# The second attention's exponentials turned by VectorE's 32x32 squares and a trip through HBM, in place of TensorE's transposes

## The chip, the core and the metric

The kernel runs on one core of a Trainium2 chip. The metric is the device time of one execution in microseconds, as a median over runs. A core has five engines that work side by side, each through its own instructions in program order: TensorE (PE, matrix products), VectorE (DVE), ScalarE (ACT), GpSimd (POOL) and SyncE (SP), which here only issues DMAs. They wait for one another through semaphores.

## What is computed

Sixteen images x of 256 channels by 1024 positions. A convolutional attention block, then on the 1024 tokens t of 256 channels:

```python
xn      = group_norm(x, 8 groups) * w + b
q, k, v = split(qkv_w @ xn + qkv_b)
x       = x + proj_w @ (softmax(q^T k / 16) v) + proj_b      # first attention, 1024 x 1024
t       = tokens(x)
u       = layer_norm(t)
c       = u / |u|
t       = t + softmax((c c^T) ** 2) u                        # second attention, 1024 x 1024
t       = t + round(clip(layer_norm(t) @ sign(W) * g + bias, -1, 1) * 7) / 7
```

The scores c c^T of the second attention are symmetric, and so are their squares' exponentials, E. Only their lower triangle is computed; the upper one is its transpose.

## The kernel before

A loop runs over the 16 images, called batches (b). 1024 tokens are 8 tiles (NT) of 128 (P). Every float32 product is made of three fp32r matmuls: a "hi" part rounded to fp32r and a "lo" part, what the rounding left out; hi x hi, hi x lo and lo x hi are added. So each operand costs a copy (hi) and a subtraction (lo).

`front(b, f)` does the group norm products, the first attention, the layer norm and the second attention's scores of batch b, with the last steps of batch f = b - 1 between them; `back(b)` does the second attention's eight products. Each engine has its own `front` and `back`, which are the order of its queue, written out by hand.

First attention: eight rows of exponentials in `expo` (four slots, DEEP). For rows 0 to 6 VectorE's `e1_turn` (line 1032) transposes within squares of 32x32 into `e_turned`, which is the memory of `x_norm`; SP's `send` and `fetch` (lines 351, 361) write that to HBM and read it back into `e_back` so that the squares stand in their transposed places; ScalarE's `e1T_hi` (766) and VectorE's `e1T_lo` (1037) split it.

Second attention: row J of E has the columns 0 to (J+1)*128. TensorE's `scores2(b, u)` makes it (row 7 as two halves, u = 7 and 8), ScalarE's `exp2` squares and exponentiates it into `expo` (822, 824), VectorE's `e2_hi` (1072) casts it into `prob[:, 0]`, and GpSimd's `e2_lo` (1333, rows 0 to 6) or VectorE's `e2_last_lo` (1077, row 7) subtracts into `prob[:, 1]`. For its blocks i < J, TensorE's `turn_e2(b, J)` (565) transposes J blocks of 128x128 into the PSUM tensor `turn`; VectorE's `e2T_parts` (1083, 1085) copies and subtracts them from there into column tile J of rows 0 to J-1 of `prob`. `product2(b, n)` then sums over j the block (j, n) of `prob` with `val`: 8 j's of three matmuls of 256 or 258 columns, into one of four PSUM places. product2(0) waits for each row's low part as it comes (`p_made`, `p_last_made`), product2(n) for `pT_made` of row n. `turn_cos` (535) and `cosT_lo` (1066) make the operands of the scores. VectorE's `residual2(n)` adds product2(n) to the tokens and takes statistics; GpSimd's and ScalarE's `layer_norm2` follow.

In `back`, the next batch is begun: ScalarE's `normalise` and `norm_hi` write `x_norm` and its hi part, GpSimd's `norm_lo` (1289) the lo part, and `bias_quads` (1338) adds a bias in `e_back`. `x_tok` holds x by tokens: written early in `front` (1009), read by `residual1` (1055) for the last time before the second attention's transposes.

Of the kernel before, what the change touches and what calls it, by code (L numbers as in the profile page):

```python
# [34 lines left out]
P = 128  # L35
# [10 lines left out]
def build(nc, x, norm_w, norm_b, qkv_w, qkv_b, proj_w, proj_b, ffn_w, ffn_b, out):  # L46
# [17 lines left out]
    GROUP_OF = [g for g, (n0, n1) in enumerate(GROUPS1) for _ in range(n0, n1)]  # L64
    assert KC == 2 and N == 2 * BANK and C // GROUPS == 32
# [6 lines left out]
    with ExitStack() as ctx:  # L72
# [62 lines left out]
        e_scratch = nc.dram_tensor("e_scratch", (NT, P, N), F32).ap()  # L135
        e_in = e_scratch.rearrange("n (i j) (q f) -> n q j i f", i=SQ, q=SQ)
# [118 lines left out]
        pT_up = sem("pT_up")  # L255
        pT_hi_made = sem("pT_hi_made")
        pT_made = sem("pT_made")
# [47 lines left out]
        def turned(J):  # L305

            first = J % 2 * BANK if J <= HT else 0
            return turn[:, first:first + J * P]


        @block.sync
        def _(sp):
# [49 lines left out]

            def front(b, f):
# [20 lines left out]
            reload_quads(1)  # L384
            with sp.Fori(1, B - 1) as b:
                reload(b + 1)
                front(b, b - 1)
                reload_quads(b + 1)
            front(B - 1, B - 2)
            store(B - 1, 0)  # L390
# [6 lines left out]
        def _(pe):  # L397
# [160 lines left out]
            def turn_e2(b, J):  # L558
                if J < 3:
                    pe.wait_ge(eT_last_made, b + 1)  # L560
                else:
                    pe.wait_ge(pT_made, (NT - 1) * b + (J - 2 if J <= HT else J - 1))
                pe.wait_ge(e2_made, NP * b + (J + 1 if J < NT - 1 else NP))
                for i in range(J):
                    mm = pe.transpose(turned(J)[:, tile(i)], expo[:, J % DEEP, tile(i)], ident[:, :])
                mm.then_inc(pT_up, 1)

            def product2(b, n):
# [7 lines left out]
                if n:  # L576
                    pe.wait_ge(pT_made, (NT - 1) * b + n)
                else:
                    pe.wait_ge(val_made, N1 * b + N1)
                def block_parts(j):  # L580
                    if n == 0 and j < NT - 1:
                        pe.wait_ge(p_made, (NT - 1) * b + j + 1)
                    elif n in (0, HT) and j == NT - 1:
                        pe.wait_ge(p_last_made, 2 * b + 1 + n // HT)
                    return prob[:, 0, j, tile(n)], prob[:, 1, j, tile(n)]

                mm = product(out2[n % 4], block_parts,
                             lambda j: val[:, j, 0:C + 2], lambda j: val[:, j, C + 2:2 * C + 2])
# [27 lines left out]
            def front(b, f, more):  # L616
# [96 lines left out]
            for n in range(NT - 2):  # L713
                product2(f, n)
                if n == 2:
                    turn_e2(f, NT - 1)
            pe.wait_ge(pT_made, (NT - 1) * B)
# [12 lines left out]
        def _(act):  # L730
            def normalise(b, k, again):
                act.wait_ge(gn_scale, b + 1)
                if again:
                    act.wait_ge(e1_written[k], 16 * SENT_OF[k] * b)
# [75 lines left out]
            def exp2(b, u):  # L810
# [8 lines left out]
                if J > DEEP:  # L819
                    act.wait_ge(pT_up, (NT - 1) * b + J - DEEP)  # L820
# [3 lines left out]
                act.activation(e, e, ACT.Exp).then_inc(e2_made, 1)  # L824

# [14 lines left out]
            def front(b, f, more, reuse=True):  # L840
# [81 lines left out]
            f = B - 1  # L922
            for n in range(NT - 3):
# [507 lines left out]
```

## Time and profile before

| | us |
|---|---|
| median of 3 runs (1765.05 to 1765.96) | 1765.87 |
| the profiled execution, its own time | 1766.2 |
| span of its core, first to last instruction | 1764.5 |
| TensorE busy | 1727.6 |
| VectorE busy | 1385.3 |
| ScalarE busy | 935.3 |
| GpSimd busy | 769.2 |

Times of single instructions come from this one profiled execution. Busy times of pipelined matmuls overlap each other, so the time that a run of them takes is read start to start from the timeline. An engine's idle time is listed with what ended it. The timeline rows used are of the batch that runs from 881.0 to 988.9 us; the batches between the first and the last look alike.

### The profile page before, as it was taken

The page shows a single profiled execution, that of the slowest core. Times are in us where ns is not written, and L with a number is a line of the kernel's source. Part 1 is how long each engine was busy: PE and PEld are TensorE (multiplying, and loading weights), DVE is VectorE, ACT ScalarE, POOL GpSimd, SP SyncE. Part 2 cuts the span into 40 slices and gives each one's busy share as a digit, 9 for nine tenths or more (in the row PEclk, how much of TensorE's full clock was granted, in tenths as well). Part 3 has the DMA queues.
Part 4 walks back from the last instruction along what each step waited for, and adds up shares of the span by engine and source line. Part 5 has one row for each costly group of instructions (what it writes and reads, how often), then busy time and mean ns, then how long its engine had stood idle before and what let it go on. Part 6 is the DMA issues. An engine that isn't in the chain of part 4 may idle for free.

```text
span 1764.5 us, 34002 instructions
## 1 busy us (share of the span) xinstructions
PE 1727.6 (98%) x11682; PEld 1578.8 (89%) x11682; DVE 1385.3 (79%) x2597; ACT 935.3 (53%) x1444; POOL 769.2 (44%) x1206
## 2 busy tenths in 40 slices
PE   7999999999999999999999999999999999999997
PEld 5898989989899998999989999898998989999896
DVE  7778877788777887778788787887778877788775
ACT  3555646455464554735547365564645546455472
POOL 1362615427154372634626246271552715437161
PEclk9999999999999999999999999999999999999998
DMA  4604315042250613406133160431504325061320
GB/s 129 167 25 137 103 51 163 24 157 81 75 139 24 186 52 100 114 36 195 31 121 95 58 178 24 135 103 50 164 24 155 83 74 140 24 187 28 103 90 25
DMA packets 139551, 169.67 MB, mean 96 GB/s; under 512 B 13184, under 2 KB 121088, under 8 KB 139520
## 3 DMA queue, kind: packets, MB, share of 16 engines
q1 hardware_dynamic: 139520, 169.27, 32.6%
q8 instruction: 18, 0.29, 0.1%
q14 instruction: 13, 0.11, 0.0%
HBM read 93.72 MB, written 75.50 MB: 96 GB/s over the span
## 4 chain that ended last, share of the span: by engine, by line
issue 27%; POOL 26%; PE 25%; DVE 7%; ACT 7%; DMA 6%; SPq 1%; POOLq 1%; DVEq 0%; ACTq 0%
PE wide L402 12%; POOL xn_lo L1289 4%; POOL ln_r L1299 4%; POOL prob L1333 4%; POOL e_back L1338 3%; PE turn L604 3%; DMA e_scratch<-x_norm 3%; DMA e_back<-e_scratch 3%; PE narrow L402 2%; POOL val L1325 2%; ACT expo L759 2%; PE turn L595 2%; POOL sq_root L1313 1%; DVE x_norm L1032 1%; DVE prob L1015 1%
## 5 line engine op out<-in xcount | busy, mean ns | idle before, releaser
L402 PE MATMUL wide<-xn_hi,prob 128*128 128x512 f32 x1024 | 305.5, 400 | 3.1 <-DVE prob L1015 3.1
L800 ACT ACTIVATE ln<-tok,ln_shift,ln_r 128x256 f32<-128x256 f32 x128 | 68.4, 592 | 303.8 <-POOL ln_shift L1301 303.8
L402 PEld LDWEIGHTS wide<-xn_hi,prob 128*128 128x128 f32 x1024 | 185.5, 188 | 44.7 <-DVE prob L1015 6.4
L1296 POOL TENSOR_TENSOR ln_v<-ln_mv,ln_eps 128x2 f32<-128x2 f32 (+1 forms) x112 | 22.1, 198 | 417.4 <-DVE ln_mv L1060 234.7
L1349 POOL TENSOR_TENSOR carrier_p<-ones 128x1 f32<-128x1 f32 x60 | 11.7, 195 | 417.2 <-DVE y_sb L1108 414.7
L766 ACT ACTIVATE prob<-e_back 128x1024 fp32r<-128x1024 f32 x112 | 118.3, 1056 | 139.6 <-DMA e_back<-e_scratch 139.6
L759 ACT ACTIVATE expo<-wide,neg_max 128x1024 f32<-128x1024 f32 x128 | 142.5, 1113 | 73.9 <-DVE neg_max L1025 73.3
L1032 DVE STREAM_TRANSPOSE x_norm<-expo 128x1024 f32<-128x1024 f32 x112 | 139.2, 1243 | 41.1 <-ACT expo L759 40.6
L1333 POOL TENSOR_TENSOR prob<-expo,prob 128x128 fp32r<-128x128 f32 (+6 forms) x112 | 148.6, 1339 | 45.8 <-DVE prob L1072 45.8
L1025 DVE TENSOR_REDUCE neg_max<-wide 128x1 f32<-128x1024 f32 x128 | 155.3, 1214 | 13.5 <-PE wide L402 11.7
L1037 DVE TENSOR_TENSOR prob<-e_back,prob 128x1024 fp32r<-128x1024 f32 x112 | 136.1, 1215 | 33.5 <-ACT prob L766 33.5
L402 PE MATMUL wide<-xn_lo,prob 128*128 128x512 f32 x512 | 160.7, 394 | 0.0
L495 PE MATMUL narrow<-val,prob 128*128 128x258 f32 x512 | 150.1, 293 | 0.0
L495 PE MATMUL narrow<-prob 128*128 128x256 f32 x512 | 147.7, 289 | 1.7 <-DVE prob L1037 1.7
L495 PE MATMUL wide<-prob 128*128 128x256 f32 x512 | 148.7, 290 | 0.0
L495 PE MATMUL wide<-val,prob 128*128 128x258 f32 x512 | 147.0, 287 | 0.0
L497 PE MATMUL narrow<-prob 128*128 128x256 f32 x512 | 145.4, 284 | 0.0
L496 PE MATMUL narrow<-prob 128*128 128x256 f32 x512 | 145.3, 284 | 0.0
L497 PE MATMUL wide<-val,prob 128*128 128x258 f32 x512 | 145.0, 283 | 0.0
L497 PE MATMUL narrow<-val,prob 128*128 128x258 f32 x512 | 144.9, 283 | 0.0
L497 PE MATMUL wide<-prob 128*128 128x256 f32 x512 | 144.8, 283 | 0.0
L496 PE MATMUL wide<-prob 128*128 128x256 f32 x512 | 144.7, 283 | 0.0
(179 smaller groups left out, 5488.9 us busy)
## 6 DMA issues: line engine op xcount, KB each, us to landing
e_scratch<-x_norm SPq DMA_DIRECT2D x112, 512.0 KB, 3.0
e_back<-e_scratch SPq DMA_DIRECT2D x448, 128.0 KB, 3.2
x_raw<-in_x SPq DMA_DIRECT2D x32, 512.0 KB, 3.7
e_back<-in_x SPq DMA_DIRECT2D x64, 256.0 KB, 5.0
out<-y_sb SPq DMA_DIRECT2D x64, 256.0 KB, 3.0
tok<-in_L_conv_qkv_w SPq DMA_DIRECT2D x1, 768.0 KB, 6.4
ln<-in_L_conv_proj_w SPq DMA_DIRECT2D x1, 256.0 KB, 6.4
ln<-in_L_ffn_weight SPq DMA_DIRECT2D x1, 256.0 KB, 3.7
```

Of the source, the lines that this page charges most:

```text
L402: mm = pe.matmul(o, lhsT, r, start=first and i == 0, stop=last and i == len(parts) - 1)
L495: pe.matmul(o[:, 0:w], hi, value_hi(j), start=j == 0, stop=False)
L496: pe.matmul(o[:, 0:C], hi, value_lo(j), start=False, stop=False, skip_group_check=True)
L497: mm = pe.matmul(o[:, 0:w], lo, value_hi(j), start=False, stop=j == NT - 1)
L759: act.activation(expo[:, n % DEEP], wide[n % 2][:, :], ACT.Exp, bias=neg_max[:, n:n + 1], accum_out=row_sum1[:, n:n + 1]).then_inc(e1_made, 1)
L766: act.activation(eT_hi[n].rearrange("p (n i t) -> p n i t", n=NT, i=SQ), e_back[:, n % 2].rearrange("p i (n t) -> p n i t", n=NT), ACT.Cop ...
L1025: dve.tensor_reduce(neg_max[:, n:n + 1], wide[n % 2][:, :], AX.X, ALU.max, negate=True).then_inc(max_made, 1)
L1032: dve.transpose(e_turned[:, n % 2].rearrange("p (q n t) -> p n q t", q=SQ, n=NT), expo[:, n % DEEP].rearrange("p (n q t) -> p n q t", q=SQ ...
L1037: dve.tensor_sub(eT_lo[n].rearrange("p (n i t) -> p n i t", n=NT, i=SQ), e_back[:, n % 2].rearrange("p i (n t) -> p n i t", n=NT), eT_hi[n ...
L1289: pool.tensor_sub(xn_lo[:, k], x_norm[:, k], xn_hi[:, k].bitcast(F32)).then_inc(xn_lo_made, 1)
L1299: pool.tensor_tensor(inv[:, cols], v[:, cols], minus_half[:, one], ALU.pow).then_inc(steps, 1)
L1333: pool.tensor_sub(prob[:, 1, J, row], expo[:, J % DEEP, row], prob[:, 0, J, row].bitcast(F32)).then_inc(p_made, 1)
```

## The change

TensorE's `turn_e2`, the PSUM reads of `e2T_parts` and their semaphores go. In their place, for rows J = 1 to 7 in five groups (1, 2), (3, 4), (5), (6), (7): VectorE's `e2_turn(b, J)` transposes the J blocks of `expo` within squares of 32x32 into a slot of `e_turned`; SP's `send2` writes a group to HBM and `fetch2` reads it back in four pieces of 32 partitions into `e2_back`, a slot in the memory of `x_tok`; ScalarE's `e2T_hi` and VectorE's `e2T_lo` split it into `prob`. Groups use two slots in turn; a fetch from the third group on waits until the slot's last group is split. `product2` waits, for j < n, for the group of row n. Its matmuls are otherwise the same, with j in the order 0 to 7 for every n. `normalise` of the next batch waits until the last group of its slot is written, as it overwrites `e_turned`, and stands among the `e2T_hi` in ScalarE's order. Left out below are declarations of semaphores and the first and last batch's copies of the same orders.

```diff
     GROUP_OF = [g for g, (n0, n1) in enumerate(GROUPS1) for _ in range(n0, n1)]
+    E2G = [(1, 2), (3, 4), (5,), (6,), (7,)]
+    E2_OF = [len(E2G) // 2, (len(E2G) + 1) // 2]
...
         e_scratch = nc.dram_tensor("e_scratch", (NT, P, N), F32).ap()
+        e2_scratch = nc.dram_tensor("e2_scratch", (len(E2G), P, (NT - 1) * P), F32).ap()
+        e2_flat = x_tok[:, :, :].rearrange("p n c -> p (n c)")
...
-        def turned(J):
-
-            first = J % 2 * BANK if J <= HT else 0
-            return turn[:, first:first + J * P]
...
+        def e2_count(b, g):
+
+            return E2_OF[e2_slot(g)] * b + g // 2 + 1
...
+        def e2_sent(g):
+
+            return e_turned[:, e2_slot(g), 0:e2_width(g) * P]
+
+        def e2_back(g):
+
+            first = e2_slot(g) * N
+            return e2_flat[:, first:first + e2_width(g) * P]
...
+            def send2(b, g):
+                sp.wait_ge(e2_turned, (NT - 1) * b + E2G[g][-1])
+                sp.dma_start(e2_scratch[g, :, 0:e2_width(g) * P], e2_sent(g)).then_inc(e2_written[e2_slot(g)], 16)
+
+            def fetch2(b, g):
+                due = 16 * e2_count(b, g)
+                sp.wait_ge(e2_written[e2_slot(g)], due)
+                if g >= 2:
+                    sp.wait_ge(e2T_made[e2_slot(g)], due)
+                source = e2_scratch[g, :, 0:e2_width(g) * P].rearrange("(i t) (q f) -> q t i f", t=Q, q=SQ)
+                back = e2_back(g).rearrange("p (i f) -> p i f", i=SQ)
+                for q in range(SQ):
+                    sp.dma_start(back[q * Q:(q + 1) * Q], source[q]).then_inc(e2_landed[e2_slot(g)], 16)
+
+            def second(b):
+                send2(b, 0)
+                fetch2(b, 0)
+                send2(b, 1)
+                send2(b, 2)
+                fetch2(b, 1)
+                send2(b, 3)
+                fetch2(b, 2)
+                send2(b, 4)
+                fetch2(b, 3)
+                fetch2(b, 4)
...
-            def turn_e2(b, J):
-                if J < 3:
-                    pe.wait_ge(eT_last_made, b + 1)
-                else:
-                    pe.wait_ge(pT_made, (NT - 1) * b + (J - 2 if J <= HT else J - 1))
-                pe.wait_ge(e2_made, NP * b + (J + 1 if J < NT - 1 else NP))
-                for i in range(J):
-                    mm = pe.transpose(turned(J)[:, tile(i)], expo[:, J % DEEP, tile(i)], ident[:, :])
-                mm.then_inc(pT_up, 1)
+            def product2_parts(b, n, j, order):
+                if j < n:
+                    g = E2G_OF[n]
+                    pe.wait_ge(e2T_made[e2_slot(g)], 16 * (e2_count(b, g) + 1))
+                hi, lo = prob[:, 0, j, tile(n)], prob[:, 1, j, tile(n)]
+                w = C + 2
+                o = out2[n % 4]
+                pe.matmul(o[:, 0:w], hi, val[:, j, 0:w], start=j == order[0], stop=False)
+                pe.matmul(o[:, 0:C], hi, val[:, j, w:w + C], start=False, stop=False, skip_group_check=True)
+                return pe.matmul(o[:, 0:w], lo, val[:, j, 0:w], start=False, stop=j == order[-1])
...
-                if n:
-                    pe.wait_ge(pT_made, (NT - 1) * b + n)
-                else:
                     pe.wait_ge(val_made, N1 * b + N1)
-                def block_parts(j):
+                if n == HT:
+                    pe.wait_ge(p_last_made, 2 * b + 2)
+                for j in range(NT):
                     if n == 0 and j < NT - 1:
                         pe.wait_ge(p_made, (NT - 1) * b + j + 1)
-                    elif n in (0, HT) and j == NT - 1:
-                        pe.wait_ge(p_last_made, 2 * b + 1 + n // HT)
-                    return prob[:, 0, j, tile(n)], prob[:, 1, j, tile(n)]
-
-                mm = product(out2[n % 4], block_parts,
-                             lambda j: val[:, j, 0:C + 2], lambda j: val[:, j, C + 2:2 * C + 2])
+                    elif n == 0:
+                        pe.wait_ge(p_last_made, 2 * b + 1)
+                    mm = product2_parts(b, n, j, range(NT))
...
                 scores2(b, 3)
-                turn_e2(b, 1)
-                turn_e2(b, 2)
                 scores2(b, 4)
-                turn_e2(b, 3)
                 turn_cos(b, 3)
                 scores2(b, 5)
-                turn_e2(b, 4)
                 scores2(b, 6)
-                turn_e2(b, 5)
                 scores2(b, 7)
                 scores2(b, 8)
-                turn_e2(b, 6)
...
                 for n in range(NT):
                     product2(b, n)
-                    if n == 2:
-                        turn_e2(b, NT - 1)
...
             def normalise(b, k, again):
                 act.wait_ge(gn_scale, b + 1)
                 if again:
-                    act.wait_ge(e1_written[k], 16 * SENT_OF[k] * b)
+                    act.wait_ge(e2_written[k], 16 * E2_OF[k] * b)
                 act.activation(by_tile(x_norm[:, k]), by_quad(x_raw[:, k]), ACT.Identity, bias=gn_b[:, k:k + 1],
                                scale=gn_a[:, k:k + 1]).then_inc(xn_made, 1)
...
                 if J > DEEP:
-                    act.wait_ge(pT_up, (NT - 1) * b + J - DEEP)
+                    act.wait_ge(e2_turned, (NT - 1) * b + J - DEEP)
...
+            def e2T_hi(b, J):
+                g, m = E2G_OF[J], e2_first(J)
+                act.wait_ge(e2_landed[e2_slot(g)], 16 * SQ * e2_count(b, g))
+                back = e2_back(g).rearrange("p (i n t) -> p n i t", i=SQ, t=Q)[:, m:m + J]
+                act.activation(prob[:, 0, 0:J, tile(J)].rearrange("p n (i t) -> p n i t", i=SQ), back, ACT.Copy
+                               ).then_inc(e2T_hi_made, 1)
...
                 exp2(b, 6)
                 exp2(b, 7)
                 exp2(b, 8)
+                e2T_hi(b, 1)
+                e2T_hi(b, 2)
 
             def back(b, more):
-                if more:
-                    for k in range(KC):
-                        normalise(b + 1, k, again=True)
-                        norm_hi(b + 1, k, again=True)
+                e2T_hi(b, 3)
+                e2T_hi(b, 4)
+                normalise(b + 1, 0, again=True)
+                norm_hi(b + 1, 0, again=True)
+                e2T_hi(b, 5)
+                normalise(b + 1, 1, again=True)
+                norm_hi(b + 1, 1, again=True)
+                e2T_hi(b, 6)
+                e2T_hi(b, 7)
...
+            for J in range(3, NT):
+                e2T_hi(f, J)
...
-            def e2T_parts(b, J):
-                up = turned(J).rearrange("p (i t) -> p i t", i=J)
-                dve.wait_ge(pT_up, (NT - 1) * b + J)
-                dve.tensor_copy(prob[:, 0, 0:J, tile(J)], up).then_inc(pT_hi_made, 1)
-                dve.wait_ge(pT_hi_made, (NT - 1) * b + J)
-                dve.tensor_sub(prob[:, 1, 0:J, tile(J)], up, prob[:, 0, 0:J, tile(J)].bitcast(F32)
-                               ).then_inc(pT_made, 1)
+            def e2_turn(b, J):
+                g, m = E2G_OF[J], e2_first(J)
+                dve.wait_ge(e2_made, NP * b + (J + 1 if J < NT - 1 else NP))
+                if g < 2:
+                    dve.wait_ge(e1_written[e2_slot(g)], 16 * SENT_OF[e2_slot(g)] * (b + 1))
+                else:
+                    dve.wait_ge(e2_written[e2_slot(g)], 16 * (e2_count(b, g) - 1))
+                dve.transpose(e2_sent(g).rearrange("p (q n t) -> p n q t", q=SQ, t=Q)[:, m:m + J],
+                              expo[:, J % DEEP, 0:J * P].rearrange("p (n q t) -> p n q t", q=SQ, t=Q)
+                              ).then_inc(e2_turned, 1)
+
+            def e2T_lo(b, J):
+                g, m = E2G_OF[J], e2_first(J)
+                dve.wait_ge(e2T_hi_made, (NT - 1) * b + J)
+                back = e2_back(g).rearrange("p (i n t) -> p n i t", i=SQ, t=Q)[:, m:m + J]
+                low = dve.tensor_sub(prob[:, 1, 0:J, tile(J)].rearrange("p n (i t) -> p n i t", i=SQ), back,
+                                     prob[:, 0, 0:J, tile(J)].rearrange("p n (i t) -> p n i t", i=SQ).bitcast(F32))
+                if J == E2G[g][-1]:
+                    low.then_inc(e2T_made[e2_slot(g)], 16)
...
                 cosT_lo(b, 2)
+                e2_turn(b, 1)
                 e2_hi(b, 2)
-                e2T_parts(b, 1)
-                e2T_parts(b, 2)
+                e2_turn(b, 2)
                 e2_hi(b, 3)
+                e2_turn(b, 3)
                 cosT_lo(b, 3)
-                e2T_parts(b, 3)
                 e2_hi(b, 4)
-                e2T_parts(b, 4)
+                e2_turn(b, 4)
                 e2_hi(b, 5)
-                e2T_parts(b, 5)
+                e2_turn(b, 5)
                 e2_hi(b, 6)
+                e2_turn(b, 6)
                 e2_hi(b, 7)
                 e2_last_lo(b, 7)
-                e2T_parts(b, 6)
                 e2_hi(b, 8)
+                e2_turn(b, 7)
+                e2T_lo(b, 1)
+                e2T_lo(b, 2)
                 e2_last_lo(b, 8)
 
             def back(b):
-                for n in range(NT):
-                    if n == 2:
-                        e2T_parts(b, NT - 1)
+                e2T_lo(b, 3)
+                e2T_lo(b, 4)
+                residual2(b, 0)
+                residual2(b, 1)
+                e2T_lo(b, 5)
+                residual2(b, 2)
```

## Rows read from the trace of the kernel before

**Rows 1.** The page, part 1 (busy us, share, instructions) and clock by slices.

```profile
PE 1727.6 (98%) x11682; PEld 1578.8 (89%) x11682; DVE 1385.3 (79%) x2597; ACT 935.3 (53%) x1444; POOL 769.2 (44%) x1206
...
PEclk9999999999999999999999999999999999999998
```

**Rows 2.** Groups of instructions by shape: busy us, mean ns, idle before.

```profile
L565 PE MATMUL turn<-ident,expo 128*128 128x128 f32 x448 | 64.5, 272 | 0.0
```

**Rows 3.** Timeline, TensorE, one batch: start us, length us, engine, line, op, out<-in.

```profile
881.00 0.62 PE L402 MATMUL wide<-xn_hi,qk_lo 128*128 128x512 f32 x2
...
954.40 0.49 PE L565 MATMUL turn<-ident,expo 128*128 128x128 f32 x3
...
955.18 0.63 PE L535 MATMUL narrow<-ident,cos_x 128*128 128x128 f32 x4 [0.30 <-ACT cos_x L795]
...
963.95 0.82 PE L565 MATMUL turn<-ident,expo 128*128 128x128 f32 x6
964.52 0.37 PE L495 MATMUL narrow<-val,prob 128*128 128x258 f32 x1
...
967.42 0.39 PE L495 MATMUL narrow<-val,prob 128*128 128x258 f32 x1
...
967.88 0.28 PE L495 MATMUL narrow<-val,prob 128*128 128x258 f32 x1
...
973.66 0.93 PE L565 MATMUL turn<-ident,expo 128*128 128x128 f32 x7
...
988.87 0.62 PE L402 MATMUL wide<-xn_hi,qk_lo 128*128 128x512 f32 x2
```

**Rows 4.** Timeline, VectorE, same batch.

```profile
958.59 0.48 DVE L1072 CAST prob<-expo 128x640 fp32r<-128x640 f32 x1
...
960.31 0.82 DVE L1072 CAST prob<-expo 128x768 fp32r<-128x768 f32 x1
...
962.99 1.83 DVE L1072 CAST prob<-expo 128x896 fp32r<-128x896 f32 x2
964.86 2.51 DVE L1077 TENSOR_TENSOR prob<-expo,prob 128x512 fp32r<-128x512 f32 x1
```

**Rows 5.** Timeline, VectorE, last batch.

```profile
1724.00 0.69 DVE L1077 TENSOR_TENSOR prob<-expo,prob 128x512 fp32r<-128x512 f32 x1
```

**Rows 6.** Timeline, GpSimd, same batch.

```profile
955.22 2.46 POOL L1333 TENSOR_TENSOR prob<-expo,prob 128x384 fp32r<-128x384 f32 x2
959.15 1.57 POOL L1333 TENSOR_TENSOR prob<-expo,prob 128x640 fp32r<-128x640 f32 x1 [1.47 <-DVE prob L1072]
960.68 1.51 POOL L1325 TENSOR_TENSOR val<-ln_x,val 128x512 fp32r<-128x512 f32 x1
962.15 1.85 POOL L1333 TENSOR_TENSOR prob<-expo,prob 128x768 fp32r<-128x768 f32 x1
964.57 2.24 POOL L1333 TENSOR_TENSOR prob<-expo,prob 128x896 fp32r<-128x896 f32 x1 [0.56 <-DVE prob L1072]
```

**Rows 7.** Timeline, ScalarE, same batch as rows 3.

```profile
960.85 0.92 ACT L822 ACTIVATE expo<-wide 128x896 f32<-128x896 f32 x1 [1.22 <-PE wide L402]
```

**Rows 8.** Groups by shape: square transposes, xn_lo, bias.

```profile
L1032 DVE STREAM_TRANSPOSE x_norm<-expo 128x1024 f32<-128x1024 f32 x112 | 139.2, 1243 | 41.1 <-ACT expo L759 40.6
...
L1289 POOL TENSOR_TENSOR xn_lo<-x_norm,xn_hi 128x1024 fp32r<-128x1024 f32 x30 | 74.2, 2495 | 14.6 <-ACT xn_hi L742 14.6
...
L1338 POOL TENSOR_TENSOR e_back<-e_back,quad_bias 128x1024 f32<-128x1024 f32 x32 | 67.2, 2120 | 8.4 <-DVE quad_bias L1130 8.4
```

**Rows 9.** The page, part 6: DMA issues, KB each, us from issue to landing.

```profile
e_scratch<-x_norm SPq DMA_DIRECT2D x112, 512.0 KB, 3.0
e_back<-e_scratch SPq DMA_DIRECT2D x448, 128.0 KB, 3.2
```

**Rows 10.** Stretches of prologue and tail: us, busy PE, PEld, DVE, ACT, POOL (instructions), clock, DMA.

```profile
25.00:26.00 1.00, 0.00 (x0) 0.00 (x0) 0.96 (x3) 1.00 (x1) 0.07 (x1) 1.00 0.00 0
1747.00:1751.00 4.00, 1.35 (x11) 0.87 (x9) 1.00 (x2) 3.33 (x5) 0.22 (x2) 1.00 0.00 0
1751.50:1754.50 3.00, 2.53 (x6) 2.04 (x7) 2.86 (x5) 0.00 (x0) 0.00 (x0) 0.50 0.00 0
```

More of the change, by code:

```diff
@@ L64, in build @@
     GROUP_OF = [g for g, (n0, n1) in enumerate(GROUPS1) for _ in range(n0, n1)]
+    E2G = [(1, 2), (3, 4), (5,), (6,), (7,)]
+    E2_OF = [len(E2G) // 2, (len(E2G) + 1) // 2]
+    E2G_OF = {J: g for g, rows in enumerate(E2G) for J in rows}
     assert KC == 2 and N == 2 * BANK and C // GROUPS == 32
@@ L254, in build @@
         p_last_made = sem("p_last_made")
-        pT_up = sem("pT_up")
-        pT_hi_made = sem("pT_hi_made")
-        pT_made = sem("pT_made")
+        e2_turned = sem("e2_turned")
+        e2_written = [sem("e2_written0"), sem("e2_written1")]
+        e2_landed = [sem("e2_landed0"), sem("e2_landed1")]
+        e2T_hi_made = sem("e2T_hi_made")
+        e2T_made = [sem("e2T_made0"), sem("e2T_made1")]
         pv2_up = sem("pv2_up")
@@ L303, in offset, with e2_slot, e2_width, e2_first @@
             return P if (J + 1) * P == BANK + P else 0
-        def turned(J):
-            first = J % 2 * BANK if J <= HT else 0
-            return turn[:, first:first + J * P]
+        def e2_slot(g):
+            return (g + 1) % 2
+        def e2_count(b, g):
+            return E2_OF[e2_slot(g)] * b + g // 2 + 1
+        def e2_width(g):
+            return sum(E2G[g])
+        def e2_first(J):
+            return sum(i for i in E2G[E2G_OF[J]] if i < J)
+        def e2_sent(g):
[3 more added lines that the diff above has]
+            return e2_flat[:, first:first + e2_width(g) * P]
         @block.sync
@@ L384, in _ @@
             reload_quads(1)
+            second(0)
             with sp.Fori(1, B - 1) as b:
@@ L388, in _ @@
                 reload_quads(b + 1)
+                second(b)
             front(B - 1, B - 2)
+            second(B - 1)
             store(B - 1, 0)
@@ L714, in _ @@
                 product2(f, n)
-                if n == 2:
-                    turn_e2(f, NT - 1)
-            pe.wait_ge(pT_made, (NT - 1) * B)
             turn_ln2(f, 0, LAST)
@@ L1198, in front @@
                 cosT_lo(b, 2)
+                e2_turn(b, 1)
                 e2_hi(b, 2)
-                e2T_parts(b, 1)
-                e2T_parts(b, 2)
+                e2_turn(b, 2)
                 e2_hi(b, 3)
+                e2_turn(b, 3)
                 cosT_lo(b, 3)
-                e2T_parts(b, 3)
                 e2_hi(b, 4)
-                e2T_parts(b, 4)
+                e2_turn(b, 4)
                 e2_hi(b, 5)
-                e2T_parts(b, 5)
+                e2_turn(b, 5)
                 e2_hi(b, 6)
+                e2_turn(b, 6)
                 e2_hi(b, 7)
                 e2_last_lo(b, 7)
-                e2T_parts(b, 6)
                 e2_hi(b, 8)
+                e2_turn(b, 7)
+                e2T_lo(b, 1)
+                e2T_lo(b, 2)
                 e2_last_lo(b, 8)
             def back(b):
-                for n in range(NT):
-                    if n == 2:
-                        e2T_parts(b, NT - 1)
+                e2T_lo(b, 3)
[4 more added lines that the diff above has]
+                residual2(b, 2)
+                e2T_lo(b, 6)
+                residual2(b, 3)
+                e2T_lo(b, 7)
+                for n in range(HT, NT):
                     residual2(b, n)
@@ L1233, in _ @@
             f = B - 1
-            for n in range(NT - 2):
-                if n == 2:
-                    e2T_parts(f, NT - 1)
-                residual2(f, n)
+            e2T_lo(f, 3)
+            e2T_lo(f, 4)
+            residual2(f, 0)
+            residual2(f, 1)
+            e2T_lo(f, 5)
+            residual2(f, 2)
+            e2T_lo(f, 6)
+            residual2(f, 3)
+            e2T_lo(f, 7)
+            residual2(f, 4)
+            residual2(f, 5)
             ln2T_lo(f, 0, LAST)
@@ L1255, in prepare @@
                 pool.memset(half[:, :], 0.5).then_inc(eT_made[1], 16)
-                pool.memset(minus_one[:, :], -1.0)
-                pool.memset(ln_eps[:, :], LN_EPS)
+                pool.memset(minus_one[:, :], -1.0).then_inc(e2T_made[0], 16)
+                pool.memset(ln_eps[:, :], LN_EPS).then_inc(e2T_made[1], 16)
                 pool.memset(norm_eps[:, :], NORM_EPS)
```

## The prediction

> **What bounds the kernel now.** Busy time first: TensorE is busy 98% of the span, VectorE 79% [rows 1]. The granted clock is 9 tenths or more except in the last slice [rows 1]. So TensorE's own work is the span, as long as it stays fed. Then the group that the change deletes: 448 transposes, 64.5 us of busy time [rows 2]. They are pipelined, so busy time overstates them; the timeline of one batch gives their true price. Its queries start at 881.00, those of the next at 988.87: a period of 107.9 us [rows 3]. Last I read who is late around those transposes, on each engine, because an instruction taken out of TensorE's queue gives time back only where the next one is ready.
>
> **What the deleted transposes really cost TensorE.** Start to start, six take 964.52 - 963.95 = 0.57 us, 0.095 each [rows 3]. 28 per batch are 2.7 us, with some 0.08 for the restart of the matmul behind each of six blocks 3.2 us. Over 16 batches 51 us: the number that a reader of the busy table would expect.
>
> **Where it is not given back.** (a) Blocks J=1 and 2 stand before score row 4, and block J=3 (954.40) before turn_cos(3), which still idled 0.30 us for ScalarE's cos_x and started at 955.18 [rows 3]. ScalarE's order up to there isn't touched, so turn_cos(3) stays where it is and the first three blocks give nothing. (b) Blocks 4, 5 and 6, 15 transposes, give 15 x 0.095 and restarts, about 1.55 us: product2(0) starts at about 962.95 in place of 964.52 [rows 3]. But product2(0) needs in its last steps e2_lo(6) (GpSimd) and e2_last_lo(7) (VectorE); at present its eighth step starts at 967.42, right behind the VectorE op that ends at 964.86 + 2.51 = 967.37 [rows 3, 4]. (c) Only the block of seven, from 973.66, lies in a stretch where TensorE is the only limit. From product2(1)'s start to the next queries is 988.87 - 967.88 = 20.99 us; seven products of 24 matmuls at 0.12 are 20.2. So 0.79 us returns there.
>
> **The chain that decides: the lows of rows 4 to 7.** VectorE and GpSimd hold each other up where VectorE casts from SBUF or subtracts with both operands in SBUF. e2_last_lo of 512 columns takes 0.69 us with GpSimd idle [rows 5] and 2.51 us beside e2_lo(6), ending 0.56 us after GpSimd does at 964.57 + 2.24 = 966.81 [rows 4, 6]. The cast of row 6 started at 962.99, waited until e2_lo(5) ended at 964.00, and e2_lo(6) followed at 964.57.
>
> Now the new order. e2_hi(4) stands directly behind cosT_lo(3); it is held only by e2_lo(2) and (3), which end at 955.22 + 2.46 = 957.68, and ends at 958.1, where at present it begins at 958.59 [rows 4, 6]. So e2_lo(4) starts at 958.2, not 959.15: ends 959.75. e2_hi(5), ready at 959.65, goes first then: 960.2. value_lo(3): 961.25 (1.06 after the cast, as before). e2_lo(5), 1.85 us: 963.05 [rows 6]. e2_hi(6): its exponential is done at about 962.3 (ScalarE starts it at 960.85, right behind score row 6 [rows 7]; now 0.44 earlier, 1.9 long), so e2_lo(5) decides: 963.55. e2_lo(6), 2.24: 965.85. Here the change puts e2_turn(6) between e2_hi(6) and e2_hi(7). A square transpose of 1024 columns takes 1.243 us [rows 8]; with 0.07 fixed and 0.135 per 128 columns, as issued back to back (an estimate; no shorter one is in the trace), row 6 costs 0.88 and row 7 1.02. So e2_hi(7) arrives at 964.4, when GpSimd is in e2_lo(6), and waits until 965.85. At present it slips in ahead of e2_lo(6). Then e2_hi(7), e2_last_lo(7): 966.8. product2(0) ends at 967.3, against 967.88: 0.6 us earlier.
>
> **What product2(1) now waits for.** It needs the group of rows 1 and 2 back and split. The data are there: e2_turn(2), early in VectorE's order, is done by about 953.3, a write takes 3.0 us and a read 3.2 [rows 9], with four issues about 8.5 us, landed by 962. But e2T_lo(1) and (2) stand in VectorE's order behind e2_hi(8) and e2_turn(7): 966.7 + 0.34 + 1.02 + 0.21 + 0.42 gives 968.7. So product2(1) starts at 968.75, 0.87 us later than before. With the 0.79 of (c), the batch is longer by about 0.1 us. Of the 3.2 us nothing is left; TensorE is idle instead: 0.8 before the seventh step of product2(0), 0.55 before the eighth, 1.45 before product2(1), 2.8 us of 3.65 from 965.1 to 968.75.
>
> **What else moves, and its cover.** The seven copies of the squares' upper parts go from VectorE to ScalarE; VectorE gets seven transposes of nearly the same length for them: load about level. The low parts now read SBUF, so they can be held by GpSimd's xn_lo (2.5 us) and bias (2.1 us) [rows 8]. Worked through with trip times as above: rows 3, 4 done at 970.4 (needed 974.5); row 5's fetch waits for the slot that e2T_lo(2) frees at 968.7, lands 973.2, done 974.7 (needed 980.3); row 6 done 979.5 (needed 983.2); row 7, whose fetch waits for row 5's slot, lands at 979.1, ScalarE 980.1, VectorE held by the bias op 982.6 (needed 986.1). Least slack 3.4 us: costed at nothing. normalise of the next batch waits for the last write (about 973.9); xn_lo ends near 978.7 against 989: nothing. On SP the x reload follows the last fetch (976.4), needed 20 us later. ScalarE's and GpSimd's last layer norm rows stay tied to product2(7). The 28 more waits before matmuls of product2 are on passed semaphores; product2(0) has eight such waits now at a pitch of 0.12 us: nothing.
>
> The Trainium skill (VectorE: DVE Perf Modes, "Rules for kernel authors") speaks against this edit: it sends a 128x128 transpose to TensorE where PSUM will do, and leaves VectorE its 32x32 squares. TensorE's 0.095 us [rows 3] stand against 0.15 of VectorE per block of 128 columns [rows 8]; by the rule the change loses, by TensorE's busy row it gains 51 us, and the sum above lies near zero.
>
> **The clock.** A gap of this form has a price that the middle of this trace doesn't show. In the tail TensorE was busy 1.35 us of the 4 us from 1747, and then ran at half the clock (1.2 GHz) in the whole stretch 1751.5 to 1754.5 [rows 10]. In the prologue it was idle for the whole microsecond 25 to 26 and kept 2.4 GHz [rows 10]. The new gap (0.85 busy of 3.65) is emptier than the first and lies inside steady work, once per batch. Half clock for some 3.2 us loses about 1.6 us of TensorE's time, in the products, where it is the limit. Whether it falls in a given batch I take as even: the bounds are no batch (nothing) and 16 batches (26 us); half, 8 x 1.6 = 13 us, because the two rows bracket the gap from both sides.
>
> The Trainium skill (TensorE: Matmul & The Clock Gate, "What's actually happening") says that the slow clock is the default and activity releases it; the tail's rows agree.
>
> **Sum.** Profiled execution of before: span 1764.5, 1766.2 with what lies around it, 0.3 above the median 1765.87. + 16 x 0.1 + 13 = 1780.8; less 0.3: 1780 us.
>
> **Rivals.**
> 1. Same chain, clock stays up: 1764 to 1770, so 1767. For it: gaps of 1 us didn't lower it; against it: 1747 to 1754.5.
> 2. The gap is shorter: if VectorE's chain ends up to 1 us earlier (e2_hi(7) let in before e2_lo(6), or faster transposes), product2(1) starts with product2(0)'s end. 16 x 1 less: 1750. Against it: GpSimd is released by e2_hi(6) itself, 0.9 us before e2_hi(7) can arrive.
> 3. All of it comes back: 1766 - 51 = 1715. It needs VectorE and GpSimd to be off the path, which [rows 3, 4] refute.
> 4. Slower by the trip: the four-piece reads have runs of 384 to 896 bytes, and two trips stand in a row behind e2T_lo(2) (rows 5, then 7). From 1.7 us extra on each trip on, product2(7) waits; at 3 us each it waits 2.6 us, + 42: some 1810 without a clock fall. For it: no row shows so short a run; against it: e_back's 3.2.
>
> **How the numbers follow.** Forecast (gap and clock falls) 0.48, 1772 to 1792; rival 1 0.20; rival 2 0.13; rival 3 0.03; rival 4 0.16. Range 1760 to 1798: the forecast, rival 1, the near part of 2 and of 4, about 0.8. A measurement can tell about 0.2%, 3.5 us, from no change: faster 0.16, same 0.17 (most of rival 1), slower 0.67. Both signs are open only through VectorE's order, so the forecast's own range, 1772 to 1792, is the one to hold it to.
>
> **What would show it.** TensorE's transposes of expo in PSUM fall from 448 to none; product2(0)'s first step at -1.5 us against the scores' start, its last near -0.6; idle before product2(1) near 1.4 us released by VectorE's e2T_lo, in every batch; e2_hi(7) waiting behind e2_lo(6). Clock of some batches at one half for 3 us just behind that gap. No wait of product2(3), (5), (6), (7). It is wrong if product2(1) isn't late, if the clock stays up, or if products 5 to 7 wait for landings.

## The result, and the profile after

The changed kernel takes 1790.53 us (median of four, 1789.10 to 1791.13), the kernel before 1765.46 on the same chip: 1.0141 of it, 95% interval 1.0124 to 1.0159. It is 25 us slower, though TensorE has less to do. The page of the changed kernel, part 1, beside [rows 1]:

```profile
PE 1707.2 (95%) x11234; PEld 1551.0 (87%) x11234; DVE 1347.9 (75%) x2597; ACT 996.2 (56%) x1556; POOL 778.3 (44%) x1206
```

The 448 transposes are gone (11682 to 11234 matmuls), TensorE is busy 20 us less and its share fell from 98 to 95%. In the span of 1788.4 us its waits have new names. From the list of waits of the changed kernel (who waited for whom: total us, times, longest):

```profile
PE narrow L619 <- DVE prob L1151: 20.1, 16, 1.3
...
PE narrow L619 <- POOL prob L1418: 8.6, 16, 0.6
PE wide L456 <- DVE tokT_lo L1122: 8.6, 16, 0.7
...
PE narrow L619 <- DVE prob L1133: 6.2, 16, 0.4
```

Line 1151 is e2T_lo, 1418 e2_lo, 1133 e2_last_lo. Each of these three comes 16 times, once per batch, 34.9 us together. (Line 1122 is cosT_lo; it is taken up under part (a) below.) The timeline of one batch shows where. Its queries start at 892.93, 11.93 us later than those of the batch in [rows 3], so 11.93 is to be taken off to compare. TensorE:

```profile
892.93 0.62 PE L456 MATMUL wide<-xn_hi,qk_lo 128*128 128x512 f32 x2
...
974.92 0.28 PE L619 MATMUL narrow<-val,prob 128*128 128x258 f32 x1
...
976.96 0.28 PE L621 MATMUL narrow<-val,prob 128*128 128x258 f32 x1
977.74 0.39 PE L619 MATMUL narrow<-val,prob 128*128 128x258 f32 x1 [0.51 <-POOL prob L1418]
...
978.09 0.28 PE L621 MATMUL narrow<-val,prob 128*128 128x258 f32 x1
978.75 0.39 PE L619 MATMUL narrow<-val,prob 128*128 128x258 f32 x1 [0.39 <-DVE prob L1133]
...
979.09 0.28 PE L621 MATMUL narrow<-val,prob 128*128 128x258 f32 x1
980.62 0.58 PE L619 MATMUL narrow<-val,prob 128*128 128x258 f32 x1 [1.24 <-DVE prob L1151]
981.00 0.41 PE L620 MATMUL narrow<-val,prob 128*128 128x256 f32 x1
...
1002.21 0.62 PE L456 MATMUL wide<-xn_hi,qk_lo 128*128 128x512 f32 x2
```

product2(0) starts at 974.92, which is 962.99 on the old batch's clock, 1.5 us earlier than in [rows 3]. product2(1) starts at 980.62, which is 968.69 on the old batch's clock, where [rows 3] has 967.88. And its first matmuls take 0.41 us where 0.28 is usual. GpSimd and VectorE in the same stretch, beside [rows 4, 6]:

```profile
969.94 1.56 POOL L1418 TENSOR_TENSOR prob<-expo,prob 128x640 fp32r<-128x640 f32 x1 [0.43 <-DVE prob L1128]
971.47 1.19 POOL L1410 TENSOR_TENSOR val<-ln_x,val 128x512 fp32r<-128x512 f32 x1
973.15 1.85 POOL L1418 TENSOR_TENSOR prob<-expo,prob 128x768 fp32r<-128x768 f32 x1 [0.49 <-DVE prob L1128]
975.57 2.12 POOL L1418 TENSOR_TENSOR prob<-expo,prob 128x896 fp32r<-128x896 f32 x1 [0.56 <-DVE prob L1128]
```

```profile
974.29 1.19 DVE L1128 CAST prob<-expo 128x896 fp32r<-128x896 f32 x1 [0.47 <-ACT expo L864]
975.41 0.96 DVE L1143 STREAM_TRANSPOSE x_norm<-expo 128x768 f32<-128x768 f32 x1
976.30 1.67 DVE L1128 CAST prob<-expo 128x512 fp32r<-128x512 f32 x1
978.00 0.69 DVE L1133 TENSOR_TENSOR prob<-expo,prob 128x512 fp32r<-128x512 f32 x1
978.61 0.42 DVE L1128 CAST prob<-expo 128x512 fp32r<-128x512 f32 x1
978.95 1.10 DVE L1143 STREAM_TRANSPOSE x_norm<-expo 128x896 f32<-128x896 f32 x1
979.98 0.58 DVE L1151 TENSOR_TENSOR prob<-x_tok,prob 128x128 fp32r<-128x128 f32 x2
```

The cast of row 7's first half (976.30) takes 1.67 us, where the same cast takes 0.42 at 978.61: e2_lo(6) on GpSimd runs beside the first until 977.69 and beside the second not at all. Behind it stand the subtraction, a cast, the transpose of row 7, and only then the two lows that product2(1) needs. ScalarE had delivered their hi parts long before:

```profile
976.47 0.60 ACT L870 ACTIVATE prob<-x_tok 128x128 fp32r<-128x128 f32 x2
```

The clock, in stretches of the changed kernel (columns as in rows 10):

```profile
980.00:980.50 0.50, 0.00 (x0) 0.00 (x0) 0.50 (x4) 0.50 (x1) 0.00 (x0) 0.62 0.00 0
980.60:983.20 2.60, 2.58 (x12) 2.59 (x13) 2.53 (x6) 1.14 (x2) 1.27 (x1) 0.50 0.44 96
```

Here it falls in the middle of the idle time before product2(1), at 980.12, and stays at 1.2 GHz for 3.4 us, 2.9 of them in work. Each of the first fifteen batches has a fall close to this place: in the first it begins 1.0 us after product2(1)'s start, then earlier from batch to batch, and from the eighth on about 0.5 us ahead of it. In the fifteenth the clock stays low for 6.8 us. In the sixteenth the three waits are there and the clock doesn't fall. The kernel before has no fall in the second attention; its only ones are at 51.6 us, in the first batch, and in the tail. From one batch's queries to the next's it is 107.8 to 107.9 us before (107.2 the first) and 109.2 to 109.5 after (110.8 the fifteenth).

### The profile page after: what moved, and what is told of

Same layout as the page of the kernel before. It is cut to its first block, busy times and chain, and to the rows that moved or that the text cites. A ratio compares the mean times of both kernels' runs of the same rounds, so it can differ in the third digit from the quotient of the medians.

```text
span 1788.4 us, 33803 instructions
## 1 busy us (share of the span) xinstructions
PE 1707.2 (95%) x11234; PEld 1551.0 (87%) x11234; DVE 1347.9 (75%) x2597; ACT 996.2 (56%) x1556; POOL 778.3 (44%) x1206
## 4 chain that ended last, share of the span: by engine, by line
issue 29%; POOL 25%; PE 22%; DVE 8%; ACT 7%; DMA 6%; SPq 1%; POOLq 1%; DVEq 0%; ACTq 0%
PE wide L456 11%; POOL e_back L1423 4%; POOL ln_r L1384 4%; POOL prob L1418 3%; PE turn L655 3%; DMA e_back<-e_scratch 3%; POOL val L1410 3%; DMA e_scratch<-x_norm 3%; PE narrow L456 2%; ACT expo L799 2%; POOL xn_lo L1374 2%; PE turn L646 2%; DVE x_norm L1088 1%; POOL sq_root L1398 1%; DVE prob L1071 1%
## 5 line engine op out<-in xcount | busy, mean ns | idle before, releaser
L619 PE MATMUL narrow<-val,prob 128*128 128x258 f32 x512 | 161.0, 315 | 34.9 <-DVE prob L1151 20.1
L1081 DVE TENSOR_REDUCE neg_max<-wide 128x1 f32<-128x1024 f32 x128 | 155.2, 1213 | 12.0 <-PE wide L456 10.8
L620 PE MATMUL narrow<-val,prob 128*128 128x256 f32 x512 | 154.2, 301 | 0.0
L621 PE MATMUL narrow<-val,prob 128*128 128x258 f32 x512 | 154.2, 301 | 0.0
L549 PE MATMUL narrow<-prob 128*128 128x256 f32 x512 | 147.3, 288 | 2.5 <-DVE prob L1093 2.5
L549 PE MATMUL wide<-prob 128*128 128x256 f32 x512 | 148.7, 290 | 0.0
L619 PEld LDWEIGHTS narrow<-val,prob 128*128 128x128 f32 x512 | 107.7, 210 | 45.3 <-DVE prob L1151 20.3
L1128 DVE CAST prob<-expo 128x128 fp32r<-128x128 f32 (+2 forms) x144 | 118.3, 831 | 36.5 <-ACT expo L864 36.5
L551 PE MATMUL narrow<-prob 128*128 128x256 f32 x512 | 144.8, 283 | 0.0
```

Source lines behind the costliest of these rows:

```text
L549: pe.matmul(o[:, 0:w], hi, value_hi(j), start=j == 0, stop=False)
L551: mm = pe.matmul(o[:, 0:w], lo, value_hi(j), start=False, stop=j == NT - 1)
L619: pe.matmul(o[:, 0:w], hi, val[:, j, 0:w], start=j == order[0], stop=False)
L620: pe.matmul(o[:, 0:C], hi, val[:, j, w:w + C], start=False, stop=False, skip_group_check=True)
L621: return pe.matmul(o[:, 0:w], lo, val[:, j, 0:w], start=False, stop=j == order[-1])
L1081: dve.tensor_reduce(neg_max[:, n:n + 1], wide[n % 2][:, :], AX.X, ALU.max, negate=True).then_inc(max_made, 1)
```

## Experiments

The theory: TensorE's time that the transposes took was time in which it would have waited for GpSimd and VectorE; what is new is a wait for VectorE's order before product2(1), and the gap costs a clock fall on top. Rivals: the clock is innocent; the trip through HBM comes late; busy time counts after all. The first four ran on one chip beside the kernel before (1764.60 there).

**The gap filled.** In the changed kernel, matmuls that nobody reads, where TensorE idled:

```diff
+                def fill(count):
+                    for _ in range(count):
+                        pe.matmul(turn[:, 0:C], prob[:, 0, 0, tile(0)], val[:, 0, 0:C], start=True, stop=True)
+                if n == 1:
+                    fill(11)
                 for j in range(NT):
+                    if n == 0 and j in (NT - 2, NT - 1):
+                        fill(6 if j == NT - 2 else 4)
```

> The changed kernel, with 21 extra matmuls of 256 columns per batch whose result nobody reads, placed in TensorE's queue where it idled: 6 before the seventh step of product2(0), 4 before the eighth, 11 before product2(1) (each 0.12 us, 2.5 us in all). No wait and no result changes. Theory (the gap lowers TensorE's clock in every batch, 1.4 us each): TensorE stays busy, the clock stays up, the period goes from 109.3 to about 107.9 us and the time to some 1767 us, though TensorE does more work. Rival (the clock is harmless, the 1.4 us per batch are waits or slower steps elsewhere): no shorter than 1790, and up to 40 us longer if the extra matmuls don't fit in the idle time.

Measured: 1769.15 us (1768.52 to 1770.62), 1.0027 of before, interval 1.0017 to 1.0038. With 336 matmuls more it is some 21 us faster than the changed kernel, and the waits for lines 1151, 1418 and 1133 are gone from its list. Period 108.0 us, and the granted clock is 1.00 from the first batch until the tail. From the first queries to the last, fifteen periods, it takes 22.7 us less than the changed kernel: that is what sixteen low stretches of 3.4 us cost, 1.4 each. And it takes 1.9 us more than before, 0.12 per batch: that is what the change costs without the clock. It is a low figure, as before has a fall in its first batch and this kernel has none; from the second batch on the periods are 107.8 and 108.0, a difference of 0.16.

**The two lows ahead.** One move in VectorE's order:

```diff
                 e2_last_lo(b, 7)
+                e2T_lo(b, 1)
+                e2T_lo(b, 2)
                 e2_hi(b, 8)
                 e2_turn(b, 7)
-                e2T_lo(b, 1)
-                e2T_lo(b, 2)
                 e2_last_lo(b, 8)
```

> The changed kernel with e2T_lo(1) and e2T_lo(2) ahead of e2_hi(8) and e2_turn(7) in VectorE's order; nothing else moves. Theory (product2(1) waits for VectorE's order, not for the trip): the wait before product2(1) goes from 1.3 to about 0 us, the gap is then too small for the clock to fall, period about 106.6 us, 1744 us. If the clock still falls in every batch: 108.1 and 1769. Rival (the trip through HBM, or ScalarE's share of it, is what comes late): the wait before product2(1) stays and the time stays near 1790.

Measured: 1748.11 us (1747.23 to 1749.88), 0.9910 of before (0.9893 to 0.9926). Two lines moved make the changed kernel some 41 us faster (0.9910 of before, not 1.0141); the time is 4 us above the 1744 expected. Its list of waits:

```profile
PE narrow L619 <- POOL prob L1418: 8.7, 16, 0.7
...
PE narrow L619 <- DVE prob L1133: 6.2, 16, 0.4
```

The wait for line 1151 is gone, the other two are as they were, and the clock doesn't fall in any batch. Period 106.7 us (107.5 and 107.0 in the second and third). So the data had been there: the wait was for VectorE's order, not for the trip.

**The trip made longer.**

```diff
             def fetch2(b, g):
                 due = 16 * e2_count(b, g)
+                sp.dma_start(pad[g:g + 1, :], x_d[0, 0:1, 0, 0:P]).then_inc(padded, 16)
+                sp.wait_ge(padded, 16 * (len(E2G) * b + g + 1))
```

> The changed kernel with a small HBM to HBM copy of 512 bytes that SP issues and waits for before each of the five fetches: about 2 us more on each trip, in series with what SP does next. Theory (least slack of a landing is 3 us or more and one trip of the two in a row is not enough to use it up): period unchanged within 0.3 us, 1790 to 1795. Rival (the trips are on the path): at least 2 us per batch, 1822 or more.

Measured: 1793.14 us (1791.62 to 1796.79), 1.0170 of before (1.0153 to 1.0187), 2.6 us above the changed kernel's 1790.53. The first two delays of one batch in SP's timeline, each with the write ahead of it, the copy and the fetch:

```profile
1075.78 0.35 SPq L392 DMA_DIRECT2D e_scratch<-x_norm  x1
1076.18 0.58 SPq L396 DMA_DIRECT2D pad<-in_x  x1
1078.14 1.73 SPq L404 DMA_DIRECT2D x_tok<-e_scratch  x4
1081.09 3.68 SPq L392 DMA_DIRECT2D e_scratch<-x_norm  x2
1084.82 0.55 SPq L396 DMA_DIRECT2D pad<-in_x  x1
1086.89 1.75 SPq L404 DMA_DIRECT2D x_tok<-e_scratch  x4
```

From the copy's issue to the fetch's it is 2 us each time, but the first fetch had to wait for its write for most of that anyway. Counted from the batch's queries, the five fetches are issued 0.4, 2.0, 0.6, 3.0 and 2.5 us later than in the changed kernel, and their data land 0.3, 1.7, 0.7, 2.3 and 2.5 us later (medians over the batches). So the experiment delays three of the five trips by about 2 us, the second, fourth and fifth, and hardly the other two. TensorE's waits are those of the changed kernel (20.1, 8.7 and 6.2 us): these three trips are covered with 2 us to spare. It is not much more than that: row 7's low part, whose two trips in a row are both longer, is done 3.2 to 3.7 us before product2(7) in most batches, 2.0 to 2.1 in three of the four without a fall, where TensorE comes sooner, and 0.5 in the fourth. The expected time came true, the unchanged period did not. The periods do something new: 108.0 in four batches, 109.3 to 109.5 in seven, 110.8 in two (and 108.4 and 110.6 in the first two). In the batches of 108.0 the clock doesn't fall; in those of 110.8 it is low for 6.8 us, not 3.4. TensorE's gap is as long as ever, but it no longer lowers the clock each time. The idle time before product2(1) in two batches, and the stretch behind it:

```profile
546.77 0.39 PE L623 MATMUL narrow<-val,prob 128*128 128x258 f32 x1 [1.24 <-DVE prob L1155]
...
1091.19 0.58 PE L623 MATMUL narrow<-val,prob 128*128 128x258 f32 x1 [1.24 <-DVE prob L1155]
```

```profile
546.50:549.50 3.00, 2.73 (x22) 2.73 (x23) 2.89 (x8) 2.89 (x4) 0.00 (x0) 1.00 0.29 66
1091.00:1094.00 3.00, 2.81 (x13) 2.81 (x14) 2.89 (x9) 2.89 (x4) 0.00 (x0) 0.50 0.30 73
```

The two waits ahead of it are 0.52 and 0.38 us in the first batch, 0.51 and 0.39 in the second, so the gap is the same to 0.01 us. Behind the first the clock stays at full speed, behind the second it is at half. So within one kernel and one execution the length of the gap doesn't decide. And these batches without a fall are 1.3 to 1.5 us shorter than those with one, which shows the price of the clock a second time.

**The transposes taken out of the kernel before.** Only the first of each block is done, so upper parts are stale:

```diff
-                for i in range(J):
-                    mm = pe.transpose(turned(J)[:, tile(i)], expo[:, J % DEEP, tile(i)], ident[:, :])
+                mm = pe.transpose(turned(J)[:, tile(0)], expo[:, J % DEEP, tile(0)], ident[:, :])
```

> The kernel before with only one of each block's transposes left: 21 of 28 per batch are not done, so most of the upper parts are stale (part of the computation is left out); all waits, copies and the order stay. Theory (blocks 1 to 6 were done in time in which TensorE would have waited anyway; only the block of seven was on the path, 6 x 0.095): period 107.9 to about 107.3, some 1756 us. Rival (busy time is what counts): 16 x 21 x 0.095 = 32 us less, 1733.

Measured: 1753.80 us (1753.40 to 1755.61), 0.9943 (0.9927 to 0.9960): 10.8 us less, where 21 x 16 x 0.095 = 32 us of transposes were dropped. Period 107.1. In the place of the transposes TensorE waits for GpSimd's e2_lo, 12.4 us in 16 waits, of which the list of before has none. Two thirds of the transposes' time had been cover, as reckoned.

The next four ran on one chip beside before at 1765.11.

**The same gap, elsewhere in time.** To see why the clock fell every time, product2(5) is preceded by 8 matmuls of 256 columns (in the second run by 14), in steady work; the gap isn't touched.

```diff
+                if n == 5:
+                    for _ in range(8):
+                        pe.matmul(turn[:, 0:C], prob[:, 0, 0, tile(0)], val[:, 0, 0:C], start=True, stop=True)
```

> The changed kernel with 8 more matmuls of 256 columns (0.96 us) ahead of product2(5) in every batch, where TensorE is never idle; the gap before product2(1) is as it was. If a gap of this form lowers the clock whenever it comes: one fall in every batch again, periods 110.3, 1806 us. If the fall in every batch was a matter of where the gap lay in time from batch to batch (a period that repeated that): falls in some batches only, periods of 108.9 and 110.3 side by side, 1790 to 1804.

> As e7_add8 with 14 matmuls (1.68 us). Always a fall: periods 111.0, 1817 us. Only where the gap lies right in time: periods of 109.6 and 111.0 side by side, 1800 to 1815.

Measured, one run each: 1810.16 us with 8 and 1805.56 with 14: more work, less time. With 14 that is where the second of the two readings had it. With 8 it is above both (1806, or 1790 to 1804), with the periods side by side that the second reading asked for, but not fewer low stretches. With 8, the periods repeat in threes, 109.0, 111.7, 110.5. Three successive batches, in stretches around and behind the gap (columns as in rows 10):

```profile
548.50:551.50 3.00, 2.75 (x13) 2.75 (x14) 2.89 (x9) 1.39 (x2) 1.42 (x1) 0.50 0.43 106
551.90:555.00 3.10, 3.10 (x17) 3.10 (x16) 0.65 (x2) 2.22 (x3) 0.71 (x1) 0.52 0.76 228
660.50:664.00 3.50, 3.50 (x17) 3.50 (x18) 2.69 (x8) 1.19 (x2) 2.29 (x1) 0.52 0.61 184
770.00:774.00 4.00, 3.15 (x26) 3.15 (x27) 3.64 (x11) 2.00 (x2) 1.82 (x1) 1.00 0.43 117
```

From 548.0 on the half clock lasts 6.8 us, a batch later 3.4 us, and at 770 there is none, though the gap is in the row (3.15 busy of 4). With 14, nine of the first 15 batches have no fall (eight of them 109.6 to 109.7 long), five have one (111.0 to 111.2) and one 6.8 us of low clock (112.3). Counted in stretches of 3.4 us, the first fifteen batches have 16 in the changed kernel, 13 with e4_trip, 16 with 8 more matmuls, 7 with 14. So a gap of this form lowers the clock or not according to something other than its length, and what changes between these batches is where it lies in time; in the changed kernel it came back to a bad place in fifteen batches. What makes a place good is left open here.

**Row 6's transpose moved too.** As e2_lows_first, with e2_turn(6) behind e2_hi(7).

> As e2_lows_first, and e2_turn(6) behind e2_hi(7), so that e2_hi(7) isn't held by e2_lo(6). By the times of the prediction the 0.3 us that e2_last_lo(7) gains is given back, as e2_lo(6) starts 0.3 us later behind e2_hi(7): within 2 us of e2_lows_first. Rival (the place of e2_turn(6) matters by itself, as the prediction said): 5 us or more faster than e2_lows_first.

Measured: 1743.30 us (1741.70 to 1744.07), 0.9876 (0.9860 to 0.9893). It is 4.8 us below e2_lows_first, or 6 us with each against its own runs of before (0.9876 to 0.9910). The first expectation (within 2 us) missed; the rival, 5 us or more, fits as far as the measurement tells. Both casts together take 1.57 us, and e2_lo(6) starts before they end:

```profile
950.35 1.57 DVE L1128 CAST prob<-expo 128x896 fp32r<-128x896 f32 x2 [0.46 <-ACT expo L864]
```

```profile
951.64 2.26 POOL L1418 TENSOR_TENSOR prob<-expo,prob 128x896 fp32r<-128x896 f32 x1 [0.56 <-DVE prob L1128]
```

It starts 0.05 us later than in e2_lows_first, not 0.3, and lasts 0.14 us longer, so most of the gain stays. Period 106.4.

**Other work into the waits.** product2_parts takes its rows in any order; the first two products are interleaved.

```diff
+            def first_two(b):
+                for rows in (range(NT - 2), range(NT - 2, NT)):
+                    for n in range(2):
+                        product2(b, n, rows)
```

The calls of product2 for rows 0 and 1 give way to it. ScalarE's e2T_hi(1) and (2) stand before exp2(7), VectorE's e2T_lo(1) and (2) before e2_hi(6).

> The changed kernel with product2(0) and product2(1) interleaved: steps 0 to 5 of both, then steps 6 and 7 of both; e2T_hi(1), e2T_hi(2) ahead of exp2(7) on ScalarE, and e2T_lo(1), e2T_lo(2) ahead of e2_hi(6) on VectorE. Theory (every wait in product2(0) is one for the last two rows' low parts, and other products' work can fill it): TensorE idles less than 0.3 us there, no clock fall, 1.5 us per batch less than with e2_lows_first (1748): 1724 us. Rival (another bound is close behind: the trips of rows 6 and 7, or VectorE's order, now that TensorE comes 3 us earlier): a new wait ahead of product2(3), (6) or (7), and 1735 or more.

Measured: 1723.90 us (1722.26 to 1725.52), 0.9769 (0.9752 to 0.9785): 41 us faster than before. Period 105.1. No wait of a second-attention product is left in the list; what TensorE still waits for are cos_x (9.3 us) and cosT_lo (7.7). The clock has no fall in a second attention (one in the first batch at 50.2 us, as in the kernel before, and the tail's).

**The interleaving without the change.** The kernel before with the same first_two.

> The kernel before, transposes on TensorE and all, with product2(0) and product2(1) interleaved as in e6_interleaved: steps 0 to 5 of both, then 6 and 7 of both. Theory (the transposes fill the time in which TensorE would wait, so before has next to nothing to gain from the interleaving, 0.2 us of waits in product2(0) per batch; what e6_interleaved gains over before is the transposes' time): 1760 to 1765. Rival (the interleaving is the gain by itself, and the trip through HBM adds nothing): 1740 or less.

Measured, in a run of its own: 1759.78 us (1758.73 to 1760.48) against 1765.16, 0.9970 (0.9959 to 0.9982). So the interleaving gives 5 us by itself, and the trip through HBM, once its order is right, some 36 of the 51 that the transposes' price promised. About 11 of the rest stand in the list of waits: cosT_lo 7.7 us, where this kernel has 0.4, and cos_x 9.3, where it has 5.9.

## Why the prediction was right, point by point

The forecast was 1780 us, and 1790.53 was measured, inside the range and the forecast's own 1772 to 1792. The mechanism held in its main steps. One term, the clock's, was taken at about half of what it came to (13 us for 22.7). Its stated bounds, nothing and 26 us, hold what was measured, and so does the range; the closeness of the sum itself is not more than that.

**What the transposes cost, and where it isn't given back:** held. Dropping 21 of them gave 10.8 us (9 reckoned). Part (a), that blocks 1 to 3 give nothing, shows in the waits: turn_cos(3) starts 74.1 us after the batch's queries, 74.2 before. TensorE now waits 8.6 us in all for cosT_lo (0.5 before) and 9.0 for cos_x (5.7 before).

**The chain of the lows:** held to a tenth of a microsecond. On the changed batch's clock the sum put e2_lo(5) at 973.1 (973.15 measured), e2_lo(6) at 975.5 (975.57), its end at 977.8 (977.69), product2(1) at 980.68 (980.62). One order came out the other way: value_lo(3) went ahead of e2_hi(5) at 971.47, so that cast took 1.57 us; e2_lo(5) started when it was to, either way. The three gaps, 0.8, 0.55 and 1.45 in the sum, are 0.66, 0.54 and 1.41 from start to start, less the usual 0.12. The rows say 0.51, 0.39 and 1.24, as they count the matmul before the gap for its whole 0.28 us.

**The batch longer by 0.1 us without the clock:** 0.12 by e1_fill from first queries to last, 0.16 from the second batch on. The batches of e4_trip without a fall, 108.0 us, say the same.

**The clock:** the mechanism was right, its count was the term mis-sized. 8 falls of 1.6 us were taken, 13 us. There were 16 stretches of it in 15 batches, at 1.4 us each on the mean, since in ten of these batches the first 0.25 to 0.6 us of the half clock fell into idle time. That is 22.7 us, and with 1.9 it is the 24.5 us between the two kernels from first queries to last (the spans differ by 24.0). I had split the chance evenly from two rows; the trace of before has a better one that I didn't read: in its first batch TensorE idled 1.74 us at one place, and 1.4 us of work later the clock went down (0.60 on average from 51 to 54).

```profile
50.24 0.35 PE L495 MATMUL narrow<-prob 128*128 128x256 f32 x1 [1.74 <-DVE prob L1037]
```

```profile
51.00:54.00 3.00, 3.00 (x19) 3.00 (x18) 1.52 (x4) 2.15 (x3) 1.27 (x4) 0.60 0.61 211
```

Even that row wouldn't have settled it. The changed kernel idles 2.08 us at the same place, and its clock stays up:

```profile
49.26 0.36 PE L549 MATMUL narrow<-prob 128*128 128x256 f32 x1 [2.08 <-DVE prob L1093]
```

```profile
48.00:52.00 4.00, 2.74 (x23) 2.77 (x24) 3.44 (x4) 1.59 (x4) 0.48 (x1) 1.00 0.61 171
```

Nor would it have given the count: the same gap cost between 7 (e8_add14) and 16 stretches. Eight was inside what such a gap can do, and the wrong number for this loop, where it met the same fate fifteen times in a row.

**Cover:** held, with more room than the sum gave it. No later product waited. Row 7's low part is done at 992.30 + 1.40 = 993.70, and product2(7) starts at 999.32:

```profile
992.30 1.40 DVE L1151 TENSOR_TENSOR prob<-x_tok,prob 128x896 fp32r<-128x896 f32 x1
```

```profile
999.32 0.28 PE L619 MATMUL wide<-val,prob 128*128 128x258 f32 x1
```

That is 5.6 us to spare (3.9 in the first batch, the tightest), where the sum had 3.5; 1.3 of the difference is the clock's delay of TensorE. Rival 4's condition didn't arise: the largest groups' writes and reads, in runs of 896 bytes, took 2.6 us each, where the sum had 3.0 and 3.2, and the reads of the first group, in runs of 384 bytes, 1.9.

```profile
e_scratch<-x_norm SPq DMA_DIRECT2D x32, 448.0 KB, 2.6
x_tok<-e_scratch SPq DMA_DIRECT2D x128, 112.0 KB, 2.6
...
x_tok<-e_scratch SPq DMA_DIRECT2D x64, 48.0 KB, 1.9
```

**e2_turn(6) between the casts:** named as part of the cause; with the lows already moved it is 0.3 us per batch (e3_both); by itself it was not measured. The place of e2T_lo(1) and (2) is 1.3 (108.0 to 106.7), and the clock with it.

## What to carry to other kernels

Work on the busiest engine that fills a wait costs nothing, and taking it away gains nothing (here two thirds of the transposes): ask of each block whether the next instruction behind it is ready, and price its removal by that. An edit that moves work to another engine is as good as that engine's order: the same change was 25 us slower, 17 faster or 41 faster than before by the place of a few lines in the engines' orders. Where an edit opens a gap in TensorE's work, count the clock too, and don't take one run's period for a rule: a gap that comes once per loop pass may meet the same fate in nearly all of them.

## What was not expected of the hardware

The half clock came in doses, not in proportion to the gap: 3.4 us in most falls, 6.8 in some, in full work for nearly all of it. A loop can settle on it: the changed kernel had a fall in each of fifteen batches, its periods drawing together from 109.5 to 109.2, where e4_trip, with the same work on TensorE, has batches of 108.0 among them. Its sixteenth batch, and its 2.08 us of idle time in the prologue's end, had none. And more work can be less time: 14 matmuls instead of 8 took 4.6 us less, in one run each. Why is open; in these runs the gap's place in time and the loop's period changed together.
